# GpSimd's waits before its gathers: one for four freed places of the ring in place of one for each block

## What is computed

```python
q = (xn @ wq[l] + bq[l]).reshape(n, H, DH)      # H = 8 heads of DH = 32; k and v likewise
scores = jnp.einsum('ehd,ehd->eh', q[dst], k[src]) * scale
m = jax.ops.segment_max(scores, dst, num_segments=n)
ex = jnp.exp(scores - m[dst])
z = jax.ops.segment_sum(ex, dst, num_segments=n)
agg = jax.ops.segment_sum((ex / z[dst])[:, :, None] * v[src], dst, num_segments=n)
```

## Time and profile before

| what | us |
|---|---|
| median of 3 runs (lowest, highest) | 3951.3 (3948.37, 3951.6) |
| the profiled execution, its own time | 3945.3 |
| its span in the trace | 3943.5 |
| edge stage of layer 0, first to last gather | 329 to 1619 |
| edge stage of layer 1, first to last gather | 2077 to 3367 |
| gathers (line 725) | 1,760, mean 951 ns of POOL each |

### The profile page before, as it was taken

One profiled execution on the slowest core, in us unless ns is written; L12 is line 12 of the kernel. 1 busy time (PEld: TensorE's weight loads), 2 busy tenths in 40 slices (PEclk: granted clock), 3 DMA queues, 4 the chain that ended last, 5 costly groups with the idle time before them and its releaser, 6 DMA issues. The chain is left out here.

```text
span 3943.5 us, 37530 instructions
## 1 busy us (share of the span) xinstructions
PE 2343.8 (59%) x7257; PEld 1553.1 (39%) x7258; DVE 2487.8 (63%) x3969; ACT 1326.8 (34%) x3895; POOL 1835.6 (47%) x1938
## 2 busy tenths in 40 slices
PE   5763455555455555568882555545555555478798
PEld 3331333333233333345551333333333333256576
DVE  3653677787777777734333777777777877544433
ACT  1112344444344343312112443444444434222131
POOL 4005566666666666311006666666666666211000
PEclk8776676666766676679995766676776666689899
DMA  3225667677677666522216767667666766412111
GB/s 91 64 69 175 186 206 210 203 212 213 201 210 209 207 205 205 154 63 78 72 53 192 211 203 213 205 203 209 207 210 204 212 208 211 118 54 66 39 37 33
DMA packets 293357, 623.34 MB, mean 158 GB/s; under 512 B 51905, under 2 KB 163705, under 8 KB 293184
## 3 DMA queue, kind: packets, MB, share of 16 engines
q0 software_dynamic: 149904, 471.38, 40.8%
q1 hardware_dynamic: 143280, 150.27, 12.0%
HBM read 526.62 MB, written 94.78 MB: 158 GB/s over the span
## 5 line engine op out<-in xcount | busy, mean ns | idle before, releaser
L725 POOL DMA_INDIRECT ring<-kv_table,stage_ix x1760 | 1672.9, 951 | 987.9 <-issue 591.4
L951 PE MATMUL bank<-qs,hot_q 128*128 x1760 | 716.2, 555 | 638.3 <-issue 328.0
L964 PE MATMUL bank<-ring,hot_w 128*128 128x272 f32 x1760 | 704.3, 540 | 501.8 <-issue 295.6
L1860 DVE TENSOR_TENSOR ring<-ring,bank 128x1024 f32<-128x1024 f32 x440 | 532.6, 1210 | 548.9 <-issue 309.5
L951 PEld LDWEIGHTS bank<-qs,hot_q 128*128 128x128 f32 x1760 | 462.4, 275 | 819.9 <-issue 723.9
L964 PEld LDWEIGHTS bank<-ring,hot_w 128*128 128x128 f32 x1760 | 421.1, 259 | 768.5 <-issue 494.4
L1865 DVE TENSOR_REDUCE s<-ring 128x32 f32<-128x1024 f32 x440 | 532.8, 1211 | 4.2
L1210 ACT ACTIVATE stage_o<-bank 128x272 f32<-128x272 f32 x440 | 167.3, 385 | 507.4 <-remote 334.5
L1195 ACT ACTIVATE s<-bank 128x8 f32<-128x8 f32 x440 | 78.0, 177 | 728.5 <-remote 449.1
L1185 ACT ACTIVATE hot_q<-pos_b,row_of 128x128 f32<-128x128 bf16 x880 | 304.0, 395 | 6.8 <-issue 3.4
L1877 DVE TENSOR_TENSOR bank<-ring,bank 128x512 f32<-128x512 f32 x440 | 300.9, 684 | 0.0
(11 more groups left out here) (298 smaller groups left out, 2348.7 us busy)
## 6 DMA issues: line engine op xcount, KB each, us to landing
agg_d<-stage_o SPq DMA_DIRECT2D x440, 136.0 KB
ring<-kv_table,stage_ix POOLq DMA_INDIRECT x1760
pos_b<-rel_d SPq DMA_DIRECT2D x54, 256.0 KB
kv_table<-ring SPq DMA_DIRECT2D x50, 250.0 KB
h_dram<-ring SPq DMA_DIRECT2D x15, 625.0 KB
ring<-h_dram SPq DMA_DIRECT2D x15, 625.0 KB
q_tab<-ring SPq DMA_DIRECT2D x10, 644.5 KB
ring<-in_x_dram SPq DMA_DIRECT2D x10, 625.0 KB
```

The lines of the kernel that those rows point to most:

```text
L725: gps.indirect_dma_start(out=chunk[:, par * G + i, j, :], out_offset=None, in_=table, in_offset=bass.IndirectOffsetOnAxis(ap=stage_ix[:, p ...
L951: mm = ten.matmul(q_bank(third, i)[:, 0:QC], hot_q[:, i % 4, a * P:(a + 1) * P], qs[:, bass.ds(t * QC + a * QC, QC)], start=(a == 0), stop ...
L964: mm = ten.matmul(b_acc[i % 2][:, lo - OWN:MC], hot_w[:, i % 4, :], chunk[:, s, j, lo:ROW], start=(j == 0), stop=(j == QD // 2 - 1), skip_ ...
L1860: tt(k_, k_, q, ALU.mult).then_inc(S["q_used"], 1)
```

## The change

POOL still goes through the blocks of a group in order, with four gathers to each. Before, it waited at each block i for the sum of block i of group k-2. Now it waits at blocks 0 and 4 only, and there for the sums of blocks 3 and 7 of group k-2. `agg` counts the sums in order, so the wait for block 3 covers blocks 0 to 2. The last group, with 4 blocks, has one wait. Groups 0 and 1 stay as they are, and so do the ring, the semaphores and every other engine's program.

```diff
                     for i in range(n):
-                        if not begin:
-                            hold(pool, S["agg"], (k - 2) * G + (layer * NB + i + 1), S["pool_passed"])
+                        if not begin and i % (G // 2) == 0:
+                            hold(pool, S["agg"], (k - 2) * G + (layer * NB + i + G // 2), S["pool_passed"])
                         for j in range(QD):
```

## The result

The changed kernel takes **4113.9 us** (median of 4 runs, 4095.8 to 4120.3) against 3951.5 us before (4 runs, 3948.4 to 3956.1): ratio 1.040, 95% interval 1.037 to 1.043. It is slower, and outside the range of 3895 to 4055. The profiled execution spans 4112.5 us, 169.0 more than the 3943.5 before. The ratios in this document leave out single runs that are over 1.5% above the fastest of their kernel, so they can differ a little from the quotient of the medians.

The account below looks back on a forecast made before the run. POOL's gathers, with pauses made mostly by late signals, were taken to pace the edge stages. Waits per layer of 194.1 against 190.8 us gave +7 us for both layers: 3958 us median, range 3895 to 4055.

Parts of the forecast that it names:

- Part (1): At POOL's block waits: six of eight per group go; a wait already met costs nothing, so 0 booked.
- (2): POOL's gathers: none added, same queue; the 16 of a half group go out in one piece, 20.1 us.
- part (3): POOL's pauses: still two per group, now behind 16 gathers each, 3.42 us extra apiece; +0.17 us per group.
- part (5): Start of each layer: first wait needs block 3's sum, +9.6 us; one later pause falls away, -3.4.
- part (4): Schedule of a step: it still fits, head about 4.5 us into the run, half period 23.5 us, group 47.0.
- The paragraph on the rule: POOL at block 0: three blocks of gathers (15 us) issued later than possible, but not lost by the schedule.
- The first rival: DVE's head is held by late signals and POOL waits for it: 3.8 us per group, 4053 to 4148; chance 0.20.
- The rival that came true: The held head of DVE's step, with POOL waiting for block 7's sum: 3.8 us per group; chance 0.20.
- The third rival: POOL arrives first at block 0 and idles: +2.5 us a group, +125 in all, 4083 us; chance 0.05.

Follow-up runs that it names:

- after_again: The changed kernel once more, unaltered, against the kernel before, in a job with late signals: 4114.2 us, ratio 1.039.
- after_third: The changed kernel, unaltered, against the kernel before in a job where signals came at once: 3559.1 us, ratio 1.0035.

## Why the prediction was wrong

*Where it held.* Part (1) and (2): met waits are free, the gathers are the same ones, and the halves go out 16 in a piece; outside the held groups the pauses are 3.67 and 3.54 us as at the earlier trace rows, so part (3)'s 3.42 is right. The first wait, in part (5), is 16.21 us, where I had put it near 19.6 (19.75 in after_again):
```profile
438.30 0.95 POOL L725 DMA_INDIRECT ring<-kv_table,stage_ix  x1 [16.21 <-PE bank L964]
```

*The step that failed is in part (4)*: "Their last gather is out at y+20, the signals come, and blocks 0 to 3 of group k+2 start at x = y+23.5". The paragraph on the rule says it once more: POOL comes to block 0 "behind the 16 gathers of the half group before, and the signal it then lacks is that of block 3 already". I let every signal of PE be late once a run is 8 us old, and come through only when POOL has stopped. But some get through: the one that ended at 971.47, 14.5 us into the run, came in 0.04 us. Then POOL has nothing to stop for at block 0, the run becomes 32, and the schedule with its head 4.5 us into the run no longer exists. The head itself is not late: it starts at y + 25.3, where part (4) had y + 28. What is missing is POOL's pause before it. The first rival's own test ("the head starts some 8 us or more after the run") agrees with both cases read here: in the long one the head comes 25.3 us in, in a shorter one (resumed at 530.48 after 1.39 us) it comes at 538.88, 8.4 us in, is held 13.68 us, and POOL 15.88:
```profile
530.48 0.95 POOL L725 DMA_INDIRECT ring<-kv_table,stage_ix  x1 [1.39 <-PE bank L964]
...
566.09 0.95 POOL L725 DMA_INDIRECT ring<-kv_table,stage_ix  x1 [15.88 <-PE bank L964]
...
538.88 0.42 DVE L1892 TENSOR_TENSOR s<-s,pen 128x256 f32<-128x256 f32 x1
...
556.68 0.41 DVE L1905 TENSOR_TENSOR_SCAN f_lane<-pen_now,bank 64x128 f32<-64x128 bf16 x1 [13.68 <-PE bank L971]
```
The kernel before had a sign of this that I overlooked. In its steady group, 15.6 us into the run of 20 gathers from 926.64, ACT evacuates a sum in the middle of the run:
```profile
942.21 0.40 ACT L1210 ACTIVATE stage_o<-bank 128x272 f32<-128x272 f32 x1 [7.12 <-remote]
```
By ACT's program order that is the sum of block 2, over at 934.85: late, but not held until POOL stopped. What decides which signal gets through, and when, no run here shows.

*The rival that came true was mis-priced.* I took 3.8 us per held group from the pause of 7.51 in the earlier trace rows, where POOL still asked for an earlier block's sum. Measured: the 17 held groups have 280.0 us at block 4 and 5.7 at block 0, 285.7; at 2 x 3.42 they would have 116.3. That is **10.0 us per held group**, 169.4 in all. My sum for the waits was 2 x 194.1 = 388.2 and they cost 558.4, 170.2 more: the held groups account for all of it. That the rest comes out as summed (272.7 us against 271.9) is in part luck: the two first waits were 7 us shorter than put down, no pause fell away for part (5)'s -3.4 (461.87 and 485.29 both follow one of over 3.6 us), and three pauses of 8.1 to 8.2 us that I had not foreseen each stand in place of two ordinary ones. I had seen that POOL would then wait "for all of them", the maxima and the three last sums, and yet took the price from a row where it doesn't. Of frequency I allowed half of 50 as the end of the range; it was a third. At 10.0 us, my own half of 50 groups would have read +250, 4208 us.

*The third rival, the rule.* With signals at once the changed kernel loses 12.9 us (after_third), not the 125 I worked out for POOL arriving first. The Trainium skill (DMA: Bandwidth & Descriptors, Rules for kernel authors) has it that a DMA is to be issued early and its semaphore waited on late; the sign of after_third agrees with that, and the size here is a third of a percent. That late signals make the pauses, not PE's work, was right and is what the early jobs show most plainly.

## What to carry to other kernels

Where signals can come late, a wait does two things: it protects data, and it is a place where the engine may stop; here most of the late signals came through at such stops. Before waits are merged, ask at which of them the engine really stops now, what is held if it goes past, and price the stop from the last thing the merged wait asks for, with the longest run before it. Compare only within one job, and look first whether the effect that you reason about is there at all: here it was worth 10% of the kernel and came and went between jobs.

## What the runs showed of the hardware that was not expected

While GpSimd issued gathers, signals of finished matmuls reached their waiters early or late by the job, with the same program and 946 to 951 ns a gather: in after_third POOL went on 0.8 us behind a sum, in the late jobs waiters saw them up to 20 us late; the kernel before took 3546 or 3951 to 3976 us accordingly. The lateness stayed when the gathers' bytes fell to an eighth, and it is not strict: a signal 14.5 us into a run was seen after 0.04 us, while one of 976.15, under 5 us later, waited 19.5. Two halves of a change that cost 0.6% and 15.5% alone cost 4% together.
